# Sorted experts two by two: turned tiles and output tiles in pairs, and 32 input places

## The reference

```
h = silu(flat @ W1[e]) * (flat @ W3[e])          # 128 -> 256, for expert e
out = out + cw[:, e:e+1] * (h @ W2[e])           # cw is zero but for the row's top 2
```

## Time and profile before

| | |
|---|---|
| three runs, median (lowest, highest) | 2025.56 us (2020.61, 2027.13) |
| the profiled execution's own time | 2014.69 us |
| its span, mean granted TensorE clock | 2012.9 us, 0.879 |
| stage one: first transpose, last store | 1583.25, 1716.08 us |
| stage two: first transpose, last store | 1849.57, 1980.39 us |
| busy share of the span: PE, DVE, ACT, POOL | 79%, 56%, 42%, 28% |

### The profile page before, as it was taken

The page is one execution under the profiler, slowest core; times in us unless marked ns, Lnnn a source line. Parts: engine busy times, 40 slices in busy tenths (PEclk is TensorE's granted clock), DMA queues, the critical chain, the costliest instruction groups (busy, mean ns, idle before and its releaser), DMA issues. The chain is left out here.

```text
span 2012.9 us, 46758 instructions
## 1 busy us (share of the span) xinstructions
PE 1589.8 (79%) x16783; PEld 1167.5 (58%) x16783; DVE 1136.1 (56%) x3048; ACT 843.5 (42%) x1634; POOL 564.3 (28%) x782
## 2 busy tenths in 40 slices
PE   4788999999488879699987776888887588353992
PEld 3655666666256647478875554555554488242882
DVE  5745677777445448356644576876674343552434
ACT  2422455555211115334432344655554476001763
POOL 4111011111101103422212211133233355374554
PEclk9989899999699989799997987998897799555996
DMA  4000222221099200000001002222220242221224
GB/s 173 1 2 10 65 57 61 55 55 44 8 286 328 91 0 1 1 3 3 3 3 64 1 1 58 66 68 66 64 71 21 64 113 86 71 74 45 78 78 144
DMA packets 84684, 124.99 MB, mean 62 GB/s; under 512 B 17329, under 2 KB 70577, under 8 KB 82929
## 3 DMA queue, kind: packets, MB, share of 16 engines
q1 hardware_dynamic: 75824, 104.30, 17.8%
q0 software_dynamic: 8640, 17.78, 2.5%
HBM read 67.47 MB, written 55.59 MB: 61 GB/s over the span
## 5 line engine op out<-in xcount | busy, mean ns | idle before, releaser
L1527 DVE TENSOR_REDUCE small<-ps 128x8 f32<-128x1024 f32 (+1 forms) x256 | 312.5, 1223 | 120.8 <-PE ps L1313 70.4
L1454 ACT ACTIVATE scr<-ps 128x1024 f32<-128x1024 f32 x256 | 262.0, 1023 | 239.7 <-PE ps L1288 121.2
L244 POOL TENSOR_TENSOR rstd<-vare,neghalf 128x4 f32<-128x4 f32 (+1 forms) x72 | 63.2, 878 | 543.6 <-DVE vare L223 542.2
L2826 POOL DMA_INDIRECT results<-scr x142 | 135.9, 957 | 143.8 <-DVE scr L2815 59.3
L1326 PE MATMUL ps<-scr 128*32 128x256 f32 x2048 | 174.0, 414 | 0.2 <-ACT scr L1454 0.2
L1275 PEld LDWEIGHTS ps<-scr_r 32*128 32x128 f32 x1024 | 82.3, 195 | 156.0 <-ACT scr L1454 88.8
L1275 PE MATMUL ps<-scr_r 32*128 32x256 f32 x1024 | 136.3, 344 | 35.8 <-ACT scr L1454 21.8
L2746 PE MATMUL ps<-scr 128*128 128x128 f32 x1136 | 153.4, 279 | 1.3 <-ACT scr L2773 1.3
L1306 PE MATMUL ps<-scr_r 32*128 32x256 f32 x1024 | 137.8, 351 | 10.0 <-DMA scr_r<-scr_r 5.5
L2746 PEld LDWEIGHTS ps<-scr 128*128 128x128 f32 x1136 | 141.9, 196 | 1.6 <-issue 1.6
L1911 PE MATMUL ps<-scr 64*64 64x64 f32 x4480 | 120.0, 223 | 13.3 <-DVE scr L2201 7.1
(11 more groups left out here) (410 smaller groups left out, 3547.7 us busy)
## 6 DMA issues: line engine op xcount, KB each, us to landing
scr_r<-scr_r SPq DMA_DIRECT2D x512, 64.0 KB
rows_m<-kinds SPq DMA_DIRECT2D x8, 2064.0 KB, 30.2
rows_f<-kinds SPq DMA_DIRECT2D x8, 2064.0 KB, 74.7
scr<-results SPq DMA_DIRECT2D x32, 256.0 KB
scr<-rows_m SPq DMA_DIRECT2D x71, 64.5 KB
scr<-rows_f SPq DMA_DIRECT2D x71, 64.5 KB
scr<-in_l3m SPq DMA_DIRECT2D x1, 3072.0 KB, 11.1
results<-scr POOLq DMA_INDIRECT x142
```

What stands on the lines that cost most here:

```text
L244: pool.tensor_tensor(k.rstd[:, 0:self.J], k.vare[:, 0:self.J], k.neghalf[:, 0:self.J], ALU.pow).then_inc(self.e["rstd_ready"].sem, 1)
L1454: act.activation(PT[:, g % 2, 2 * x:2 * x + 2, :], ps[:, 4:6, :], ACT.Exp).then_inc(e["prob_ready"].sem, 1)
L1527: dve.tensor_reduce(nf[:, half, 0:blocks, at:at + 2].rearrange("p q a -> p a q"), ps[:, 2 * (p % 2):2 * (p % 2) + 2, :].rearrange("p a (q ...
L2826: pool.indirect_dma_start(results, bass.IndirectOffsetOnAxis(ap=names[:, j % IN, P:P + 1], axis=0), y[:, j % OUT, :], None).then_inc(store ...
```

## The change

Turned tiles j and j+1 (j even) go to one PSUM bank and are copied to SBUF by one ScalarE instruction; `xT` gets 8 places. Output tiles j and j+1 go to one bank too and are read by one VectorE instruction of 256 columns; `y` gets 8 places. The signals `turned`, `xt_ready` and `out_read` count pairs; the last pair has one tile. That leaves 2 banks for turned pairs, 4 for hidden tiles and 2 for output pairs. TensorE transposes five tiles ahead instead of four. VectorE reads a pair ahead of the product of the tile four past it. `xin` moves from the scratch buffer to `d.kept`, with 32 places. GpSimd still stores tile by tile.

```diff
@@ -2682,13 +2682,15 @@
     ps, cst = k.ps, k.w["const"]
     gate_up_of, down = w
-    e = k.signals(SORTED, turned=1, xt_ready=1, kept=1, gu_ready=1, act_ready=1, h_ready=1, out_ready=1, out_read=1)
-    IN, OUT, DEEP = 16, 4, 4
+    e = k.signals(SORTED, kept=1, gu_ready=1, act_ready=1, h_ready=1, out_ready=1)
+    pairs = k.signals((SORTED + 1) // 2, turned=1, xt_ready=1, out_read=1)
+    IN, XT, DEEP, OUT = TILES, 8, 4, 8
     loads = [k.signals((SORTED - n + 3) // 4, **{"load_%d" % n: 16})["load_%d" % n] for n in range(4)]
     stores = [k.signals((SORTED - n + 3) // 4, **{"scatter_%d" % n: 16})["scatter_%d" % n] for n in range(4)]
-    xin, xT, sil, hT = k.carve((IN, P + 1), (DEEP, P), (DEEP, 2 * P), (DEEP, 2 * P))
-    here, y = k.carve((DEEP, 2, 2 * P), (OUT, P), base=k.scr2[:, 6144:8704])
+    xin = d.kept
+    xT, sil, hT, y = k.carve((XT, P), (DEEP, 2 * P), (DEEP, 2 * P), (OUT, P))
+    here, = k.carve((DEEP, 2, 2 * P), base=k.scr2[:, 6144:9728])
     names = xin.bitcast(I32)
     def there(j):
@@ -2698,6 +2700,11 @@
         if there(j):
             eng.wait_ge(e[name].sem, e[name].at(j))
+    def wait_pair(eng, name, m):
+        if 0 <= m:
+            eng.wait_ge(pairs[name].sem, pairs[name].at(m))
     def landed(eng, j):
         if there(j):
@@ -2707,24 +2714,37 @@
         if there(j):
             eng.wait_ge(loads[j % 4].sem, loads[j % 4].at(j // 4))
+    def ends_pair(j):
+        return there(j) and (j % 2 == 1 or j == SORTED - 1)
+    def tiles_of(m):
+        return slice(2 * m, min(2 * m + 2, SORTED))
+    def width(m):
+        return P * (tiles_of(m).stop - 2 * m)
     def turned_at(j):
-        return ps[:, j % 3, 0:P]
+        return ps[:, j // 2 % 2, P * (j % 2):P * (j % 2) + P]
     def hidden_at(j):
-        return ps[:, 3 + j % 3, :]
+        return ps[:, 2 + j % 4, :]
     def out_at(j):
-        return ps[:, 6 + j % 2, 0:P]
+        return ps[:, 6 + j // 2 % 2, P * (j % 2):P * (j % 2) + P]
     def sp(sp):
         for j in range(SORTED):
             if load and j >= 16 and j % 4 == 0 and j < 16 + 4 * PIECES:
                 load(sp, (j - 16) // 4)
             row = sp.value_load(d.table[0:1, 1, j:j + 1], min_val=0, max_val=8 * ROWS + 6 * P)
-            wait(sp, "turned", j - IN)
+            if there(j - IN):
+                wait_pair(sp, "turned", (j - IN) // 2)
             landed(sp, j - IN)
             arrived(sp, j - 4)
             sp.dma_start(xin[:, j % IN, :], d.rows[bass.ds(row, P), :]).then_inc(loads[j % 4].sem, 16)
@@ -2734,33 +2754,37 @@
         def turn(j):
             arrived(pe, j)
-            wait(pe, "xt_ready", j - 3)
-            pe.transpose(turned_at(j), xin[:, j % IN, 0:P], cst["ident"]).then_inc(e["turned"].sem, 1)
+            if j % 2 == 0:
+                wait_pair(pe, "xt_ready", j // 2 - 2)
+            ins = pe.transpose(turned_at(j), xin[:, j % IN, 0:P], cst["ident"])
+            if ends_pair(j):
+                ins.then_inc(pairs["turned"].sem, 1)
         def gate_up(j):
-            wait(pe, "xt_ready", j)
+            wait_pair(pe, "xt_ready", j // 2)
             wait(pe, "kept", j)
-            wait(pe, "h_ready", j - 3)
+            wait(pe, "h_ready", j - 4)
             for n in range(2):
                 for c in range(2):
                     ins = pe.matmul(hidden_at(j)[:, 256 * n + P * c:256 * n + P * c + P],
-                                    here[:, j % DEEP, n, P * c:P * c + P], xT[:, j % DEEP, :], start=True, stop=True)
+                                    here[:, j % DEEP, n, P * c:P * c + P], xT[:, j % XT, :], start=True, stop=True)
             ins.then_inc(e["gu_ready"].sem, 1)
         def project(j):
             at = pe.value_load(d.table[0:1, 0, j:j + 1], min_val=0, max_val=7 * 256)
             wait(pe, "h_ready", j)
-            wait(pe, "out_read", j - 2)
+            if j % 2 == 0:
+                wait_pair(pe, "out_read", j // 2 - 2)
             for c in range(2):
                 ins = pe.matmul(out_at(j), hT[:, j % DEEP, P * c:P * c + P], down[:, bass.ds(at + P * c, P)],
                                 start=(c == 0), stop=(c == 1))
             ins.then_inc(e["out_ready"].sem, 1)
-        for j in range(-4, SORTED + 3):
+        for j in range(-5, SORTED + 3):
             if there(j):
                 gate_up(j)
-            if there(j + 4):
-                turn(j + 4)
+            if there(j + 5):
+                turn(j + 5)
             if there(j - 3):
                 project(j - 3)
@@ -2772,22 +2796,24 @@
             wait(act, "gu_ready", j - DEEP)
             act.activation(here[:, j % DEEP], gate_up_of[:, :, bass.ds(at, 256)], ACT.Copy).then_inc(e["kept"].sem, 1)
-        def keep_turned(j):
-            wait(act, "turned", j)
-            wait(act, "gu_ready", j - DEEP)
+        def keep_turned(m):
+            wait_pair(act, "turned", m)
+            wait(act, "gu_ready", 2 * m + 1 - XT)
+            dst = xT[:, 2 * m % XT:2 * m % XT + width(m) // P, :].rearrange("p n c -> p (n c)")
+            src = ps[:, m % 2, 0:width(m)]
             if affine:
-                ins = act.activation(xT[:, j % DEEP, :], turned_at(j), ACT.Identity, scale=affine[0], bias=affine[1])
+                ins = act.activation(dst, src, ACT.Identity, scale=affine[0], bias=affine[1])
             else:
-                ins = act.activation(xT[:, j % DEEP, :], turned_at(j), ACT.Copy)
-            ins.then_inc(e["xt_ready"].sem, 1)
-        for j in range(-3, SORTED):
+                ins = act.activation(dst, src, ACT.Copy)
+            ins.then_inc(pairs["xt_ready"].sem, 1)
+        for j in range(-4, SORTED):
             if j == 2:
                 d.exps(act)
             if j == 5:
                 d.gap_exps(act)
-            if there(j + 3):
-                keep_turned(j + 3)
+            if ends_pair(j + 4):
+                keep_turned((j + 4) // 2)
             if there(j):
                 wait(act, "gu_ready", j)
                 wait(act, "h_ready", j - DEEP)
@@ -2797,35 +2823,41 @@
     def dve(dve):
         d.shift(dve)
-        for j in range(SORTED + 3):
+        def write_out(m):
+            wait(dve, "out_ready", tiles_of(m).stop - 1)
+            for j in range(2 * m - OUT, 2 * m - OUT + 2):
+                landed(dve, j)
+            out = ps[:, 6 + m % 2, 0:width(m)].rearrange("p (n c) -> p n c", c=P)
+            dst = y[:, 2 * m % OUT:2 * m % OUT + width(m) // P, :]
+            if scale is None:
+                ins = dve.tensor_copy(dst, out)
+            else:
+                ins = dve.tensor_tensor(dst, out, row4(scale, width(m) // P), ALU.mult)
+            ins.then_inc(pairs["out_read"].sem, 1)
+        for j in range(SORTED + 5):
             if j == 4:
                 d.weigh(dve)
             if j == 8:
                 d.share(dve)
+            if ends_pair(j - 4):
+                write_out((j - 4) // 2)
             if there(j):
                 wait(dve, "act_ready", j)
                 wait(dve, "out_ready", j - DEEP)
                 dve.tensor_tensor(hT[:, j % DEEP, :], hidden_at(j)[:, 256:512], sil[:, j % DEEP, :],
                                   ALU.mult).then_inc(e["h_ready"].sem, 1)
-            if there(j - 3):
-                wait(dve, "out_ready", j - 3)
-                landed(dve, j - 3 - OUT)
-                out = out_at(j - 3)
-                if scale is None:
-                    ins = dve.tensor_copy(y[:, (j - 3) % OUT, :], out)
-                else:
-                    ins = dve.tensor_tensor(y[:, (j - 3) % OUT, :], out, scale, ALU.mult)
-                ins.then_inc(e["out_read"].sem, 1)
             if beside and j < TILES:
                 beside(dve, j)
     def pool(pool):
         for j in range(SORTED):
-            wait(pool, "out_read", j)
+            wait_pair(pool, "out_read", j // 2)
             landed(pool, j - 4)
             pool.indirect_dma_start(results, bass.IndirectOffsetOnAxis(ap=names[:, j % IN, P:P + 1], axis=0),
                                     y[:, j % OUT, :], None).then_inc(stores[j % 4].sem, 16)
-        for j in range(SORTED - OUT, SORTED):
+        for j in range(SORTED - 4, SORTED):
             landed(pool, j)
     k.add_phase(sp=sp, pe=pe, act=act, dve=dve, pool=pool)
```

## The result

The changed kernel takes 2042.92 us (median of 5 runs, 2037.89 to 2048.61) against 2025.56 (2020.61 to 2030.5, 5 runs in the same session): ratio 1.0092, 95% interval 1.0069 to 1.0115. The forecast was 2013 in 2000 to 2032, so both sign and range missed; "slower" had been given 0.15. The profiled execution of the changed kernel has a span of 2042.2 us.

A forecast was written before the change was run, and what follows sets the result against it. It took SyncE's row loads, slowed by closely following stores, to become the limit once the output wait went. Terms -9.0 - 7.4 + 3.9 = -12.5 us took 2014.69 to 2002.2, scaled to a 2013 us median; range 2000 to 2032.

The forecast's parts named there:

- Part 1: Paired output tiles: TensorE's wait for VectorE's output read goes; 27.7 us saved at most over both sorted stages.
- Part 2: Next loop, ScalarE's weights copy behind Silu: 3.5 us available, 1.2 needed, news 1.5 late fits; cost nothing, gain nothing.
- Part 3: SyncE's row loads become the limit; stores in twos give 1.63 us a load, saving 9.0 and 7.4 us.
- the 16.4 us that the sum took off: Savings from faster loads in the sorted stages: 9.0 us in stage two and 7.4 in stage one.
- Parts 4 and 5: 32 input places, taken as 0 (0 to 2 us); turned pairs save ScalarE 0.1 to 0.2 us a tile, mostly hidden.
- the estimate of 1.8 us for the dropped increments: 35 fewer transpose semaphore increments a stage at 26 ns, 0.9 us each stage; would lower the sum by 1.8 us.
- Part 6: Transposes five ahead: first gate_up later, +1.0 us over two stages; stage ends 1.45 us later each, +2.9.
- Rival C: Longer bursts: stores in fours slow loads to 1.87 us each; +14.3 us, so 2040; chance 0.13.
- The clause at the end: Wrong at root if loads run at 1.3 while TensorE takes 1.6 a tile; then a deeper order buys nothing.
- Rival B: Each store costs SyncE 0.64 us however grouped; loads stay at 1.79, deeper order costs 3.9: 2029; chance 0.19.
- rival A: Loads don't bind: stores in twos count as apart, loads at 1.28, TensorE's floor decides; 23.6 us saved, 2002; chance 0.22.

The follow-up runs named there:

- plain stores: Indirect stores replaced by plain GpSimd stores to consecutive rows, scatter left out: changed kernel 0.9793, kernel before 0.9827, each against the kernel before.
- three adds: Three 128x1 GpSimd adds without a drain behind each indirect store: kernel before 1.0004, changed kernel 1.0015, without paired outputs 1.0015, each against the kernel before.

## Why the prediction was wrong

- Part 1, the output wait goes: right (10.3 to 1.3 and 9.1 to 1.9 us). That this gives time back needed parts 2 and 3.
- Part 2, what is late next: **this step failed.** It put the lateness of news at 1.5 us and let it fit into 3.5. Even the earlier trace rows said more: of the two Silus that start at 1974.02 the first belongs to the gate_up that began at 1970.12, so it was 2.84 us late. I took the nearest gate_up on the timeline instead of the one with its number. The 3.5 is too much as well: with the 1.06 us that a gate_up takes in the earlier trace rows instead of 0.89 it is 3.3. And lateness is not fixed: it lasts as long as the run of stores does, 1.40 us in the median with threes, 2.73 with fours and up to 3.87. With a Silu and a copy behind it (0.39 and 0.63) that is over the 3.5 us at once, and the loop of gate_up, Silu, copy and gate_up breaks next. So the term that was put at nothing is the loss: 6.6 and 7.7 us between first and last transpose. Where the copy ran six ahead the ratio went from 1.0090 to 1.0027.
- Part 3, loads become the limit, and stores come in twos: wrong in both, and with it the 16.4 us that the sum took off. The load's lead at the end of stage two grew from 2.2 to 9.8 us. The slow loads of the earlier trace rows and the late news were two results of one cause, and I took the first for what bounds the stage. Twos did not come, since a hold of over 3 us gathers two pairs and lets both go together; with plain stores, where nothing is held, they did come in twos.
- Parts 4 and 5, the places and the turned pairs: nothing, as said. All of it without the paired outputs measured 0.9997 (0.9971 to 1.0023); the estimate of 1.8 us for the dropped increments is too small to be told in that. A turned pair takes ScalarE 558 ns, within the bounds of 452 and 904.
- Part 6, start and end of a stage: the first gate_up came 1.0 and 1.2 us later behind the first load, as said. The end took 3.0 and 3.6 us more behind the last transpose, where 1.45 a stage was put. The order is not all of it: that stretch is 14.2 us in both stages of the kernel before, 14.4 and 15.5 with all but the paired outputs, and 15.7 and 16.2 with the paired outputs alone.
- Rival C came near in size by luck: 2040 against 2042.92, with four stores in a row, and 1.87 us a load where it was 1.80. Its way was another: it let loads pay for the burst. It was given 0.13, since I held against it that stores thin out while TensorE waits for rows, and the changed kernel's TensorE did not wait for rows. The clause at the end, "then late news, not rows, was the limit", named the root, but its sign (loads at 1.3) did not show, and it expected no gain and not a loss.
- Rival B had the loads' pace, 1.79, but not the time, 2029. Its way, that each store costs SyncE 0.64 us however they are grouped, is refuted by three adds, where loads come every 1.2 to 1.3 us beside indirect stores 1.65 apart.

The sum with what was measured: one tile more in a run makes 7.33 us of four where it was 4.87 of three, so 1.83 against 1.62 a tile while the ring holds. The first 20 tiles of a stage, where stores have hardly begun, take as long as before (32.0 and 32.7 us before, 33.1 and 32.4 changed). Over the other 50 a tile takes 1.84 us in both stages of the changed kernel, as the ring says, and 1.73 and 1.68 in the kernel before, where not every run is an undisturbed three.

What stays open: by what way an indirect store that follows another holds SyncE's steps and the news of TensorE, and whether both are one thing, since at 1.51 us the first is rarer and the second is not. The runs show what takes the hold away (a gap of 1.65 us, the plain kind) and what does not (1.38 or 1.51 us, other rows), not the mechanism. No version that sends its rows where they belong came out under the kernel before by more than the noise: all but the paired outputs (0.9997) and three adds (1.0004) tie with it. The plain stores, at 0.98, show what the hold costs the kernel before, too.

## What to carry to other kernels

When several things are late beside one another, ask which of them would be early if the common cause were gone; a transfer that is slow may be slow with its user. Before two results are handed on at once, look at what the receiver does with a group of two: here the burst it makes sets how long everybody else waits, and the burst feeds itself. And a wait to be removed should be costed with the loop behind it at the longest lateness in the trace, not at one that stands at the stage's quiet end.

## What was not expected of the hardware

- Indirect stores on GpSimd that start 1.26 or 1.38 us apart stretch instructions of SyncE, register loads and moves among them, from 0.02 to 0.34 us to about 0.72, and let news of TensorE reach ScalarE 2.6 to 2.7 us late in the median of a stage with runs of four. At 1.51 us apart the long steps are fewer and the news is still 1.5 to 2.2 us late. At 1.65, and with plain stores 0.53 or 1.45 us apart, the median lateness is 0.04 to 0.11 us.
- The Trainium skill (DMA: Bandwidth & Descriptors, "SWDGE vs HWDGE vs iDMA") has transfers that SyncE issues immune to the interference on GpSimd's descriptor path. It speaks of another interference than this one, but read as widely as rival A read it, the runs disagree: beside indirect stores 40 of SyncE's 317 instructions for loads in stage one take over 0.55 us, most of them about 0.7, and beside plain ones from the same queue 1 of 322 does.
- A drain on GpSimd behind an indirect store waits for the store: GpSimd is idle for 1.86 us and starts the next one 1.2 us behind the end of the last packet, 3.07 us a store.
- A 128x1 add behind a store adds only 0.12 to 0.13 us to the gap between stores, though it takes 0.20: it fills idle time that was there (0.30 before each store, 0.16 with it).
